# Moving two small normalisation steps to later and earlier slots of a software pipeline, in a gated cross-attention and mixture-of-experts kernel

## The reference, cut to what matters

```python
x = x + tanh(g_xattn) * xattn(layernorm(x), ctx)     # q = xn Wq; sim = q k^T; softmax; attn v; Wout; layernorm with scale, bias
x = x + tanh(g_ffn) * ffn(layernorm(x))              # router logits, top 8 of 32 experts, shared expert + routed experts
```

## Time and profile before

| | |
|---|---|
| median of 3 runs | 2370.48 us |
| the profiled execution | 2374.31 us, the slowest of the three |
| its span in the trace | 2372.6 us |
| busy in the span | TensorE 2098.1 us (88%), VectorE 1807.9 (76%), ScalarE 1526.6 (64%), GpSimd 1325.0 (56%) |
| TensorE instructions | 14418 matmuls, as many weight loads |
| DMA | 710.02 MB, mean 299 GB/s |

### The profile page before, as it was taken

The page is one execution under the profiler, slowest core; times in us unless marked ns, Lnnn a source line. Parts: engine busy times, 40 slices in busy tenths (PEclk is TensorE's granted clock), DMA queues, the critical chain, the costliest instruction groups (busy, mean ns, idle before and its releaser), DMA issues. The chain is left out here.

```text
span 2372.6 us, 44646 instructions
## 1 busy us (share of the span) xinstructions
PE 2098.1 (88%) x14418; PEld 1923.3 (81%) x14418; DVE 1807.9 (76%) x4294; ACT 1526.6 (64%) x4487; POOL 1325.0 (56%) x1444
## 2 busy tenths in 40 slices
PE   7999679899999999999994899999898988889882
PEld 7888578899899899898894778898787777778772
DVE  4544357788888888888885668778898988889884
ACT  4433346677777777777772348888776777767761
POOL 1000213777777777787775500006767767767766
PEclk9999789999999999999996999999999999999996
DMA  8987489978878888888884999889999999999995
GB/s 283 326 282 265 129 284 313 320 254 273 265 260 271 270 268 270 267 270 267 267 281 155 376 377 300 297 298 361 375 361 353 367 366 342 374 350 366 372 334 163
DMA packets 385523, 710.02 MB, mean 299 GB/s; under 512 B 136427, under 2 KB 249036, under 8 KB 382828
## 3 DMA queue, kind: packets, MB, share of 16 engines
q1 hardware_dynamic: 336140, 564.50, 69.5%
q0 software_dynamic: 49152, 142.67, 17.3%
HBM read 349.16 MB, written 357.83 MB: 298 GB/s over the span
## 5 line engine op out<-in xcount | busy, mean ns | idle before, releaser
L1459 POOL DMA_INDIRECT parts<-results_dram,kept_index x512 | 544.7, 1064 | 470.7 <-DMA results_dram<-y 259.9
L771 POOL DMA_INDIRECT pages_dram<-rows,kept_index x472 | 477.8, 1012 | 145.8 <-issue 123.6
L840 ACT ACTIVATE exps<-sim,minus_max 128x78 f32<-128x78 f32 x1024 | 324.4, 392 | 76.1 <-DVE minus_max L918 76.1
L1510 ACT ACTIVATE hid_h<-hidden 128x512 fp32r<-128x512 f32 x176 | 111.2, 632 | 242.4 <-DVE hidden L1605 235.8
L840 ACT ACTIVATION_READ_ACCUMULATOR exps<-sim,minus_max 128x1 f32 x1024 | 266.1, 274 | 0.0
L1489 ACT ACTIVATE y<-yps,row_weight 128x256 f32<-128x256 f32 x640 | 248.1, 470 | 2.1 <-PE yps L132 2.1
L1658 PE MATMUL xps<-ident,xin 128*128 128x128 f32 x1280 | 174.1, 281 | 77.7 <-DVE wq_l L1529 49.3
L1658 PEld LDWEIGHTS xps<-ident,xin 128*128 128x128 f32 x1280 | 145.3, 145 | 90.0 <-issue 89.7
L130 PE MATMUL sim<-kT_h,qT_h 128*128 128x156 f32 x512 | 146.7, 287 | 43.7 <-DVE qT_l L1045 20.1
L130 PE MATMUL yps<-w_h,hid_h 128*128 128x256 f32 x640 | 181.1, 283 | 2.0 <-ACT y L1489 2.0
L131 PE MATMUL yps<-w_h,hid_l 128*128 128x256 f32 x640 | 181.6, 284 | 0.0
(11 more groups left out here) (268 smaller groups left out, 7649.8 us busy)
## 6 DMA issues: line engine op xcount, KB each, us to landing
xin<-pages_dram SPq DMA_DIRECT2D x160, 576.0 KB, 6.7
results_dram<-y SPq DMA_DIRECT2D x160, 512.0 KB, 5.1
pages_dram<-blank SPq DMA_DIRECT2D x108, 576.0 KB, 3.9
w_raw<-in_experts SPq DMA_DIRECT2D x160, 385.0 KB, 5.4
pages_dram<-blank SPq DMA_DIRECT2D x12, 1728.0 KB, 7.6
keys_h_dram<-keys_h SPq DMA_DIRECT2D x32, 624.0 KB, 5.7
keys_l_dram<-keys_l SPq DMA_DIRECT2D x32, 624.0 KB, 7.6
kT_h<-keys_h_dram SPq DMA_DIRECT2D x32, 624.0 KB, 5.6
```

The costliest lines, as they stand in the source:

```text
L771: pool.indirect_dma_start(dram["pages"], bass.IndirectOffsetOnAxis(ap=kept_index[:, at:at + 1].bitcast(U32), axis=0), buffer(batch)[:, k / ...
L840: last = act.activation(exps[u % 2][:, h, :], scores(u)[:, h // 4, h % 4, :], ACT.Exp, bias=minus_max[u][:, h:h + 1], accum_out=row_sum[u] ...
L1459: pool.indirect_dma_start(parts[t][:, k, :], None, done, bass.IndirectOffsetOnAxis(ap=kept_index[:, at:at + 1].bitcast(U32), axis=0)).then ...
L1510: act.activation(hid[s % 2][0][:, :], hidden[s % 2][:, :], ACT.Copy).then_inc(hid_hi, 1)
```

## The change

Three things move, all near the end of a step. No instruction is added or taken away.

```diff
@@ GpSimd, step
                 if 1 <= b <= B:
                     make_rstd(2, b - 1)
-                if b <= B - 3:
-                    make_rstd(0, b + 2)
                 if scatters:
                     scatter(b, range(12, 13))
                 if b == B:
                     ...
                     scatter(b, range(LAST_PICKS))
+                if b <= B - 3:
+                    make_rstd(0, b + 2)
@@ ScalarE, step
-                    if name == "PV1a" and 1 <= b <= B:
+                    if name == "Q3" and 1 <= b <= B:
                         ...
                         apply(2, buffer(b - 1)[:, :, 0:D], lambda t: x1[1 - par][:, t, :], b - 1)
@@ VectorE, step
                     if name == "T3b" and 1 <= b <= B:
                         dve.wait_ge(summed, b)
                         statistics(2, lambda t: x1[1 - par][:, t, :], b - 1)
-                    if name == "T3b" and b <= B - 3:
-                        dve.wait_ge(x_loaded, 16 * (b + 3))
-                        statistics(0, lambda t: x_in[:, t, :], b + 2)
                     ...
+                    if name == "Q3" and b <= B - 3:
+                        dve.wait_ge(x_loaded, 16 * (b + 3))
+                        statistics(0, lambda t: x_in[:, t, :], b + 2)
```

## The result

| | before | after |
|---|---|---|
| median of 11 runs each, in turn on one chip | 2367.84 us | 2387.54 us |
| their range | 2363.1 to 2374.31 | 2374.99 to 2393.7 |
| the profiled execution, and its span | 2374.31, 2372.6 | 2380.78, 2379.0 |

The change makes the kernel slower: the ratio is 1.0072, with an interval of 1.0051 to 1.0092, which is 17.0 us of 2367.84. The medians are 19.7 us apart. The forecast was 2370 with a range of 2357 to 2383, so it was wrong.

The account below looks back on a forecast made before the run. The prediction took a chain from VectorE through ScalarE's exponentials and TensorE back to VectorE to bound the attention steps. Steady steps 0.0, warm-up and end -0.5, experts' phase 0: 2370.48 - 0.5 = 2370.0 us, range 2357 to 2383.

Parts of the forecast that it names:

- The steady step: Attention phase: steps stay at 30.03 us, a change of 0.0 with bounds -0.47 to +0.3.
- The argument from step 30: First step without statistics(0), 1.14 us shorter: VectorE's work sets the chain, so moving the block ahead of the same reduction gains 0.
- 3.3 us further back: VectorE's statistics(0) block is put this much later, still ahead of the same first minus_max.
- VectorE's and TensorE's first wait: Start of a step: Q3's low part moves up by 1.14 us, so TensorE's 0.67 us wait goes; chain gain 0.
- Warm-up: Ahead of step 0 the block's 1.14 us may come off once; -0.5 us, between -1.2 and 0, with the end.
- The first rival: Near a step's end, z *= scale comes too late to hold probs; 7 to 12 us less, about 2360; chance 0.22.
- `x_res + bias` holds `probs`: Start of a step: GpSimd's late addition holds VectorE's probs, some 1.7 us and not 0.70, at cost 0.
- The second rival: Start of a step on ScalarE: apply(0) runs into the exponentials; with 0.5 us delay 9 us, about 2379; chance 0.13.
- the sign that the prediction named for it: In the profile after, ScalarE's exponentials would wait for nothing but their own engine.
- The 0.2 us of slack behind `apply(2)`: ScalarE: PV1a's high part, now behind apply(2), ends near 842.55, its low part starts at 842.76; cost 0.
- The step that failed: TensorE's 1.07 us of idling in two places becomes one wait of about 1.1 us ahead of X; cost 0.
- The third rival: TensorE's single 1.1 us wait lowers the granted clock; 26 steps at 0.9 us, 23 us, about 2394; chance 0.05.

Follow-up runs that it names:

- e4: Kernel before with only VectorE's statistics(0) moved behind normalise(0), into its idle time ahead of the third minus_max; 2355.61 us, ratio 0.9940.
- e1: Kernel after with ten additional identity transposes on TensorE ahead of X's wait for apply(0) in every step from 0 on; 2375.82 us, ratio 1.0024.
- e2: Kernel before with only VectorE's statistics(0) moved behind Q3, GpSimd and ScalarE as before; 2389.45 us, ratio 1.0078.
- e8: Kernel after, unchanged, run again for a second profile; 2392.59 us.

## Why the prediction was wrong, point by point

- **The steady step.** Forecast 30.03, measured 30.05 in 20 of the 24. The argument from step 30 (VectorE sets the chain, and moving the block within it gains nothing) holds: e4 shows that the same block beyond the reduction gains 0.74 us. The "3.3 us further back" is a distance in VectorE's list; the block starts 3.00 us ahead of the reduction where it was 5.17, so it is 2.2 us later.
- **VectorE's and TensorE's first wait.** Forecast gone, and it is gone.
- **Warm-up.** Forecast -0.5 us. Step 6 begins 1.4 us later on average, within the spread of single executions, so neither figure is shown.
- **GpSimd.** Forecast: it waits 0.8 us for the block (0.80), is 0.5 late at `make_rstd(1)` (0.51), and its shift ends 0.18 late (802.23 - 785.90 = 16.33 against 16.15: 0.18). `z` still holds `probs`: 1.38. The first rival, given 0.22, didn't come.
- **`x_res + bias` holds `probs`.** Forecast some 1.7, measured 1.53, hidden as said. The scatter of 1.32 takes 0.96 to 1.00 in the ordinary step, and in the long step, where a scatter (824.82) meets `probs` (824.63) again, 1.35. The Trainium skill (SBUF — State Buffer, Who interferes with whom) has whoever comes first keep the shared interface; the 1.53 agrees. The 1.94 of e4 doesn't, by the recorded starts: there VectorE's row starts 0.08 us ahead of GpSimd's and is the one that is held. The section's inference that such an instruction leaves descriptor generation alone doesn't agree either: 1.35 beside `probs`, 0.96 without.
- **ScalarE.** Forecast: `xn` from 0.33 us ahead of `minus_max`, exponentials not delayed. Measured 0.33, and 0.83 instead of 0.84. The second rival, given 0.13, didn't come; the sign that the prediction named for it (exponentials with no wait) can't tell, as `xn` ends just when the reduction does and the exponentials' row has no bracket, but the distance of 0.83 can. The 0.2 us of slack behind `apply(2)` was right too, but I didn't apply it to step 30, where the block is no longer there to cover it: 1.05 us, once.
- **The step that failed.** "The 1.07 us that TensorE idles in two places before become one wait of about 1.1 us ahead of `X`", at a cost of 0, since "the total idle time isn't larger than before". The wait was 1.27 to 1.35, mostly as the hand-over from ScalarE to TensorE (0.15 us) was not in the sum. And equal idle time isn't equal: in two pieces it never let the clock fall in the 48 steady steps of the two profiled executions before, in one piece it did in 13 of 72 steps. e1, where TensorE is busy through it, has no fall, and two thirds of the loss are gone: this is the cause of most of it.
- **The third rival** is what happened, and I gave it 0.05. Its form was wrong as well, 26 steps by 0.9 us. It is 4 to 5 steps by 2.65: 1.7 us of clock where I took 0.9 from the earlier trace rows, one stretch of a longer fall, and 1.1 us from a second hold of `probs`, which I hadn't thought of. Too many falls, each priced too low: 23 us forecast, 11.5 found.

What stays open: why the falls come in every fourth step of an undisturbed stretch and not in each, 2 us of what e1 leaves, and 4 us of the distance between the medians (1.3 by the ratio).

## What to carry to other kernels

Look at the longest single wait of TensorE in a step, not at the sum: an edit that gathers short waits into one of over 1 us can leave the engines' chain as it was and still cost the clock. Forecast the step length and then ask, for each edit, what happens in the steps that are not typical, as the few long steps and the last one decided here. Before a block is moved, look in the waits for the engine's own idle slot on the other side of the instruction that sets the chain; and before an instruction off the chain is moved, look which queue waits for it.

## What the runs showed that I had not expected

- The granted clock fell to 0.50 after waits of 1.27 to 1.36 us, which stand in nearly every step, in every fourth of them and not in the others; where a step with a shorter wait lay between, the next fall came later. Twice (e2, e8) it fell behind a wait for ScalarE's `z` as well, of 1.35 and 1.27 us.
- A fall that cost TensorE 1.7 us was paid with 2.65, since it moved VectorE into another phase with GpSimd.
- One chip ran the kernel before in 2821.87 us where every other measurement took 2367.84 to 2370.76. An edit that gained 1.1% elsewhere lost 4.7% there.
- GpSimd's descriptor work is held by VectorE too: a scatter of 0.96 to 1.04 us takes 1.25 to 1.35 in most cases where it runs up against a `probs`, and in the profiled execution before no scatter between 480 and 1222 us takes over 1.2 us without one.
